# The convolutions' four-row tiles: DMA from SBUF to SBUF in place of copies on ScalarE and VectorE

## The chip, the cores and the metric

One Trainium2 chip, one of its cores. The metric is the device time of one execution in microseconds; the time before is the median of three runs. All numbers are in float32. Engines are called as in the profile: PE (TensorE), ACT (ScalarE), DVE (VectorE), POOL (GpSimd), SP (SyncE, which here issues DMAs).

## The reference

The input `x` is [8, 32, 128, 128] (images, channels, rows, columns). Four residual blocks follow each other, each adding a branch of the group-normalized input (`_gn` with 32 groups, so one mean and variance for each image and channel):

```python
x = x + L0(_gn(x))   # depthwise 11x11 Gaussian blur
x = x + L1(_gn(x))   # a gate
x = x + L2(_gn(x))   # snake convolution, 9 taps moved along y
x = x + L3(_gn(x))   # deformable 3x3 convolution with modulation
```

Three of them contain a dense 3x3 convolution over 32 channels, and the change is about these alone. L1 pads by wrapping, convolves 32 to 32 channels, and uses mean and variance of the result and of its SiLU to gate the input. L2 convolves 32 to 18 channels (`w_off`), normalizes in nine groups, takes tanh of it, and the first nine channels, summed up from the middle, move the sampling rows. L3 convolves 32 to 18 channels (offsets) and 32 to 9 (modulation, through a sigmoid and a mean); the offsets say where the input is sampled.

## The kernel before

The eight images are worked on in two groups g of four (`NG` = 2, `GI` = 4). SBUF has 128 partitions, and a group's `xn` holds the normalized input with image b's 32 channels on partitions 32b to 32b+31 and the padded rows behind each other along the free dimension: 130 rows of 130 floats in the gate stage, 136 of 136 (`HP`, `PAD` = 4) in the others. Each stage is a function with a block of its own, one program for each engine, and ends with a barrier of all engines, so stages don't overlap. In order: weights and tables, `blur`, `gate_conv` for both groups, `gate_scale`; then for each group `residual`, `snake_offsets`, `snake`, `residual`, `dcn_offsets`, and `dcn_dense` or its alternative. The convolution runs in three kinds of stage: `gate_conv` (gate), `snake_offsets` (snake) and `dcn_offsets` (dcn); two groups make six stages.

**The convolution (`RowConv`, L614 on).** A matmul contracts over partitions, and 32 channels would fill only a quarter of them. So for each image b two tiles of 128 partitions are filled, `low` and `high`, each of [128, 32, 130]: partition block q of `low` (32 partitions) holds the rows top-1+q, top+3+q, ... of the image, every fourth one, 32 in all, and `high` the rows two further down. With a weight tile of [128, 64] for each of three columns dx, one output row quad comes from six matmuls: `low` writes output partitions 0 to 63 (two rows of 32 channels), `high` 64 to 127. A unit u is 4 x 128 columns, one PSUM bank; an image has `NU` = 8 units, and four banks `acc` rotate. In float32 each matmul shows as two records in the trace, 592 ns each at the higher clock, started 0.43 us after each other; the ones of `low` and `high` run side by side. Both tiles exist twice (index b % 2), so the tiles of image b+1 are filled while image b is convolved, and those of image b+2 may not be touched before image b's convolution is over (`conv_done`, counted per unit).

**The filling (`move`, L636 to L647).** For each image eight copies of [32, 32, 130] floats from image b's 32 partitions of `xn` into one partition block of `low` or `high`. Three are done by ACT (`OF_ACT`; recorded at L663 in the helper `act_copy`) and five by DVE (`OF_DVE`; recorded at L647). The lists say behind which unit of the image before each copy stands in its engine's order of work; those of image 0 come at the stage's start. PE waits for both counts (`wait_moved`).

**Around it.** In the gate stage the input is loaded by SP (L705), measured and normalized by DVE and ACT, wrapped around by DVE (`padded`), and then convolved. ACT takes each unit out of PSUM with SiLU (L776) into one of four `hid` tiles, DVE measures it (L741).

In the snake stage ACT takes each unit out of PSUM (L1024) into `raw[b % 2]`, DVE measures it (L1071), and behind units 1 and 2 of the next image the group mean, variance and coefficients of image b are worked out; ACT does root, and the two halves of tanh (`squash`, L1015), behind units 2, 3 and 5 of image b+1. Then SP stores image b with four DMAs of 9 partitions each (L982), and before ACT writes unit 0 of image b+2 it waits for that store.

In the dcn stage ACT takes each unit out twice, as it is (L1768, into `cm`) and through a sigmoid (L1770, into `sig`), DVE takes the largest absolute value of each unit of `cm` (L1797), POOL adds the column numbers (L1786, `placed`), and SP stores each half image (four units) of `cm` with four DMAs of 18 partitions (L1824) and the half's mean of the modulation with four of 4 partitions (L1817). `cm`, `sig` and `mm` exist twice, by half: ACT waits for the store of half h before it writes the first unit of half h+2.

SP issues in its written order and waits in place: what stands behind a wait is issued later. In the snake stage it waits only for tanh, in the dcn stage for `placed` and the kept means.

Of the kernel before, what the change touches and what calls it, by code (L numbers as in the profile page):

```python
# [11 lines left out]
ACT = mybir.ActivationFunctionType  # L12
AX = mybir.AxisListType

B, C, H, W = 8, 32, 128, 128
P = 128
GI = P // C
# [598 lines left out]
class RowConv:  # L616
# [8 lines left out]

    OF_ACT = [((0, 0), 0), ((0, 1), 2), ((0, 2), 4)]
    OF_DVE = [((0, 3), 0), ((1, 0), 1), ((1, 1), 2), ((1, 2), 3), ((1, 3), 4)]

    def __init__(self, s, xn, top, left, w):
        self.xn, self.top, self.left, self.w = xn, top, left, w  # L630
        self.rows = [[s.sb(f"{n}{i}", [P, self.NI, W + 2]) for i in range(2)] for n in ("low", "high")]
        self.acc = [s.ps(f"acc{i}") for i in range(self.BANKS)]
        self.moved_act, self.moved_dve = s.sem("moved_act"), s.sem("moved_dve")
        self.conv_done = s.sem("conv_done")
# [3 lines left out]

    def move(self, eng, copy, moved, share, b, u=None):

        for (high, q), after in share:
            if u is not None and u != after:
                continue
            if b >= 2:
                eng.wait_ge(self.conv_done, (b - 1) * self.NU)
            r0 = self.top - 1 + 2 * high + q
            copy(self.rows[high][b % 2][C * q:C * q + C, :, :],  # L647
                 self.xn[C * b:C * b + C, r0:r0 + 4 * self.NI - 3:4, self.left - 1:self.left + W + 1]).then_inc(moved, 1)

    def wait_moved(self, pe, b):  # L650
        pe.wait_ge(self.moved_act, (b + 1) * len(self.OF_ACT))
        pe.wait_ge(self.moved_dve, (b + 1) * len(self.OF_DVE))

    def convolve(self, pe, b, u):
# [4 lines left out]
        ins.then_inc(self.conv_done, 1)  # L659


def act_copy(act):
    return lambda o, i: act.activation(o, i, ACT.Copy)  # L663


def gate_conv(nc, k, x1, g):
# [6 lines left out]
    with ExitStack() as ctx:  # L673
        s = Space(nc, ctx, f"gateconv{g}")
# [5 lines left out]
        conv = RowConv(s, xn, 1, 1, k.w_gate)  # L680
# [21 lines left out]
        @block.sync  # L702
        def _(sp):
            for l in range(NL):
                sp.dma_start(xg[:, l * LR:(l + 1) * LR, :], x1_v[:, l * LR:(l + 1) * LR, :]).then_inc(loaded[l], 16)  # L705

        @block.vector
        def _(dve):
# [25 lines left out]

            dve.wait_ge(padded, 1)
            conv.move(dve, dve.tensor_copy, conv.moved_dve, conv.OF_DVE, 0)
            for b in range(GI):
                for u in range(conv.NU):
                    v = b * conv.NU + u
                    dve.wait_ge(hid_ready, v + 1)  # L740
                    dve.bn_stats(hst[:, b, u, :], hid[v % 4][:, :]).then_inc(hid_used, 1)  # L741
                    if b + 1 < GI:
                        conv.move(dve, dve.tensor_copy, conv.moved_dve, conv.OF_DVE, b + 1, u)
            dve.wait_ge(hid_used, GI * conv.NU)
# [15 lines left out]
        @block.scalar  # L760
        def _(act):
            act.wait_ge(var_ready, 1)
            act.activation(std[:, :], mv[:, 1:2], ACT.Sqrt, bias=k.eps[:, :]).then_inc(std_ready, 1)
            act.wait_ge(coef_ready, 1)
            v = xg[:, 0:ACT_ROWS, :]
            act.activation(v, v, ACT.Identity, bias=k.norm1[:, g, 1:2], scale=k.norm1[:, g, 0:1]).then_inc(normed, 1)

            act.wait_ge(padded, 1)
            conv.move(act, act_copy(act), conv.moved_act, conv.OF_ACT, 0)
            for b in range(GI):  # L770
                for u in range(conv.NU):
                    v = b * conv.NU + u
                    act.wait_ge(conv.conv_done, v + 1)
                    if v >= 4:
                        act.wait_ge(hid_used, v - 3)
                    act.activation(hid[v % 4][:, :], conv.bank(b, u)[:, :], ACT.Silu, bias=k.vec('L1_conv_proj_bias')).then_inc(hid_ready, 1)  # L776
                    if b + 1 < GI:
                        conv.move(act, act_copy(act), conv.moved_act, conv.OF_ACT, b + 1, u)

# [168 lines left out]
def snake_offsets(nc, k, xn, steps, g):  # L948


    with ExitStack() as ctx:
# [25 lines left out]
        @block.sync  # L977
        def _(sp):
            for b in range(GI):
                sp.wait_ge(tanh_ready, 2 * b + 2)  # L980
                for q in range(4):
                    sp.dma_start(steps[:, b, q::4, :], raw[b % 2][32 * q:32 * q + 9, :, :]).then_inc(stored, 16)  # L982
            sp.wait_ge(stored, 64 * GI)
# [23 lines left out]
        def _(act):  # L1007
# [8 lines left out]

            conv.move(act, act_copy(act), conv.moved_act, conv.OF_ACT, 0)
            for b in range(GI):
                for u in range(NU):
# [6 lines left out]
                    if b > 0 and u in (2, 3, 5):  # L1026
                        (root, lambda x: squash(x, 0), lambda x: squash(x, 1))[(2, 3, 5).index(u)](b - 1)
                    if b + 1 < GI:
                        conv.move(act, act_copy(act), conv.moved_act, conv.OF_ACT, b + 1, u)
            root(GI - 1)  # L1030
# [4 lines left out]
        def _(dve):  # L1035
# [27 lines left out]

            conv.move(dve, dve.tensor_copy, conv.moved_dve, conv.OF_DVE, 0)
            for b in range(GI):
                for u in range(NU):
                    v = b * NU + u
                    if b > 0 and u in (1, 2):
                        (spread, coefficients)[u - 1](b - 1)
                    dve.wait_ge(raw_ready, v + 1)  # L1070
                    dve.bn_stats(st[b % 2][:, u, :], raw[b % 2][:, u * conv.UI:(u + 1) * conv.UI, :].rearrange("p i w -> p (i w)")).then_inc(stats_done, 1)  # L1071
                    if b + 1 < GI:
                        conv.move(dve, dve.tensor_copy, conv.moved_dve, conv.OF_DVE, b + 1, u)
                aggregate(b)
# [618 lines left out]
def dcn_offsets(nc, k, xn, offs, g):  # L1693


    with ExitStack() as ctx:
# [54 lines left out]
        def _(act):  # L1751
# [5 lines left out]

            conv.move(act, act_copy(act), conv.moved_act, conv.OF_ACT, 0)
            for b in range(GI):
                for u in range(NU):  # L1760
# [11 lines left out]
                    if v % HU == 3 and v > HU:  # L1772
                        keep_mean(half - 1)
                    if b + 1 < GI:
                        conv.move(act, act_copy(act), conv.moved_act, conv.OF_ACT, b + 1, u)
            keep_mean(2 * GI - 1)
# [12 lines left out]
        def _(dve):  # L1789
            conv.move(dve, dve.tensor_copy, conv.moved_dve, conv.OF_DVE, 0)  # L1790
            dve.wait_ge(columns_drawn, 1)
            dve.tensor_scalar(pos[:, :], pos[:, :], k.is_x[:, :], k.place3[:, :], ALU.mult, ALU.add).then_inc(pos_ready, 1)
            for b in range(GI):
                for u in range(NU):
# [3 lines left out]
                                      apply_absolute_value=True).then_inc(far_seen, 1)  # L1798
                    if b + 1 < GI:
                        conv.move(dve, dve.tensor_copy, conv.moved_dve, conv.OF_DVE, b + 1, u)  # L1800
            dve.wait_ge(far_seen, GI * NU)
# [9 lines left out]
        def _(sp):  # L1811
            def store_mean(half):
                sp.wait_ge(mean_kept, half + 1)
                b, r0 = half // 2, half % 2 * HR
                for j in range(HU):
                    rows = slice(4 * (r0 + j * UI), 4 * (r0 + (j + 1) * UI))
                    sp.dma_start(offs[MOD, b, rows, :].rearrange("(i q) w -> q i w", q=4), mm[half % 2][32 * j:32 * j + 4, :, :]  # L1817
                                 ).then_inc(mod_stored[half % 2], 16)

            for half in range(2 * GI):  # L1820
                sp.wait_ge(placed, (half + 1) * HU)
                b, r0 = half // 2, half % 2 * HR
# [496 lines left out]
```

## Time and profile before

| | us |
|---|---|
| time before, median of 3 runs | 3729.3 |
| lowest and highest | 3715.83, 3739.62 |
| profiled execution, its own time | 3735.51 |
| its span in the trace | 3733.5 |

The profiled execution is the one that all rows are from; its time lies 6 us above the median, and 2 us of it lie around the span. Rows of a timeline begin with the start in us from the span's start and a duration in us, and end in brackets with how long the engine had been idle and what released it; `x3` means three instructions merged into one row, `SPq` is SP's issuing of DMAs. A group row ends with busy us and the mean ns of one instruction, then the idle time before them. A row of a stretch has the stretch, its length, busy us and instructions of PE, PEld, DVE, ACT and POOL, the granted TensorE clock (1.00 is 2.4 GHz, 0.50 is 1.2 GHz), the mean busy share of the 16 DMA engines and the GB/s they moved.

### The profile page before, as it was taken

Reading aid. Unit: us, or ns where it says so; the run is one execution under the profiler, and the core shown is the slowest. Engines: PE = TensorE matmul, PEld = TensorE weight load, DVE = VectorE, ACT = ScalarE, POOL = GpSimd, SP = SyncE. Lnnn points to the kernel's source line nnn. Section 1 sums busy time; section 2 is a strip of 40 time slices with the busy share of each in tenths; the row PEclk is TensorE's granted clock in tenths of the full one; section 3 lists DMA queues with packets and bytes.
Section 4 is the critical chain, followed back from the end, with each engine's and each line's share of the span. In section 5 each row is a group of like instructions: output and inputs, shape, how many; then the busy total and the mean of one; then the engine's idle time right before and its main releaser. Section 6 shows DMA issues by size and latency. Waiting matters only on the chain. (4 is left out here: it accounts for less than half of the span.)

```text
span 3733.5 us, 86265 instructions
## 1 busy us (share of the span) xinstructions
PE 2749.0 (74%) x38569; PEld 1536.9 (41%) x38569; DVE 2064.7 (55%) x2867; ACT 1830.3 (49%) x1855; POOL 1090.2 (29%) x724
## 2 busy tenths in 40 slices
PE   1773753759999265888888828599990858888888
PEld 1762221226666121444444412366660224444444
DVE  5996677735555473454554465455545734545453
ACT  1113564735555373555555556455553835555544
POOL 0220001024443145333333210344421643343331
PEclk7886976879999677889889858799995968899889
DMA  2554114011111621212112141111117111121111
GB/s 55 145 139 122 39 52 180 7 25 25 31 25 25 233 75 48 63 60 67 56 60 67 51 187 13 27 23 31 25 25 276 38 50 63 59 68 58 61 63 44
DMA packets 213124, 257.74 MB, mean 69 GB/s; under 512 B 79188, under 2 KB 141192, under 8 KB 210696
## 3 DMA queue, kind: packets, MB, share of 16 engines
q1 hardware_dynamic: 203528, 218.58, 20.5%
q0 software_dynamic: 9216, 33.56, 2.2%
q8 instruction: 304, 4.98, 0.6%
q14 instruction: 76, 0.62, 0.1%
HBM read 153.52 MB, written 98.57 MB: 68 GB/s over the span
## 5 line engine op out<-in xcount | busy, mean ns | idle before, releaser
L2037 PE MATMUL dense_spread<-dense_cp,kept_spread_yx 32*128 32x512 f32 x2432 | 564.4, 729 | 229.8 <-DVE dense_cp L2194 149.2
L1308 ACT ACTIVATE snake_samp<-snake_s 128x1024 f32<-128x1024 f32 x320 | 321.2, 1023 | 359.1 <-PE snake_s L1237 358.9
L2156 ACT ACTIVATE dense_samp<-dense_s 128x864 f32<-128x864 f32 (+1 forms) x384 | 305.8, 829 | 331.2 <-PE dense_s L2084 331.0
L2208 DVE TENSOR_TENSOR dense_hat<-dense_spread,dense_hat 128x1024 f32<-128x1024 f32 x256 | 300.8, 1215 | 277.6 <-PE dense_spread L2037 277.6
L1371 DVE TENSOR_SCALAR snake_hat<-snake_spread 128x1024 f32<-128x1024 f32 x256 | 301.5, 1219 | 205.3 <-PE snake_spread L1215 205.3
L2136 ACT ACTIVATE dense_hat<-dense_spread 128x1024 f32<-128x1024 f32 x256 | 254.9, 1022 | 304.9 <-PE dense_spread L2037 298.2
L2084 PEld LDWEIGHTS dense_s<-dense_hat,dense_xt 64*64 64x64 f32 x11264 | 273.3, 135 | 193.7 <-issue 141.1
L1237 PE MATMUL snake_s<-snake_hat,snake_xt 64*64 64x128 f32 x10240 | 337.8, 274 | 19.1 <-ACT snake_samp L1308 18.8
L2096 PE MATMUL dense_s<-dense_samp,kept_w_dcn 64*64 64x264 f32 x4608 | 342.7, 457 | 2.8 <-ACT dense_samp L2156 2.8
L2084 PE MATMUL dense_s<-dense_hat,dense_xt 64*64 64x108 f32 x11264 | 327.9, 261 | 0.5
L2037 PEld LDWEIGHTS dense_spread<-dense_cp,kept_spread_yx 32*128 32x128 f32 x2432 | 149.0, 201 | 427.6 <-DVE dense_hat L2208 211.3
L657 PE MATMUL dcnoff_acc<-dcnoff_low,kept_w_off 128*64 128x512 f32 x384 | 174.1, 608 | 199.2 <-DVE dcnoff_high L647 194.2
L1237 PEld LDWEIGHTS snake_s<-snake_hat,snake_xt 64*64 64x64 f32 x10240 | 285.2, 134 | 85.7 <-issue 42.2
L657 PE MATMUL snakeoff_acc<-snakeoff_low,kept_w_off 128*64 128x512 f32 x384 | 184.1, 640 | 139.8 <-DVE snakeoff_high L647 139.8
L2096 PEld LDWEIGHTS dense_s<-dense_samp,kept_w_dcn 64*64 64x64 f32 x4608 | 194.6, 162 | 199.0 <-issue 137.8
L1186 POOL TENSOR_TENSOR snake_step<-xn 128x1240 f32<-128x1240 f32 (+1 forms) x64 | 176.3, 2754 | 319.6 <-DVE snake_xt L1363 310.1
L657 PE MATMUL gateconv_acc<-gateconv_low,kept_gate_w_gate 128*64 128x512 f32 x384 | 169.4, 604 | 118.6 <-DVE gateconv_high L647 118.6
L2017 POOL COPY dense_step<-dense_rows 128x176 f32<-128x176 f32 x64 | 32.4, 507 | 757.8 <-DVE dense_xt L2201 757.6
L2219 DVE TENSOR_TENSOR dense_mod<-dense_s,dense_mod 128x528 f32<-128x528 f32 x64 | 45.3, 708 | 369.8 <-PE dense_s L2096 369.8
L1252 PE MATMUL snake_s<-snake_samp,kept_w_dsc 64*64 64x256 f32 x4096 | 247.4, 379 | 0.2
L1215 PE MATMUL snake_spread<-snake_rw,kept_spread_y 32*128 32x256 f32 x2048 | 152.3, 413 | 69.9 <-DMA snake_rw<-steps 59.8
L1194 POOL TENSOR_TENSOR snake_xt<-snake_xt,kept_of_pair 128x1280 f32<-128x1280 f32 x64 | 148.5, 2320 | 169.3 <-ACT snake_xt L1302 169.3
(314 smaller groups left out, 4856.7 us busy)
## 6 DMA issues: line engine op xcount, KB each, us to landing
dense_cp<-offs SPq DMA_DIRECT2D x576, 56.0 KB
x<-blur_x SPq DMA_DIRECT2D x16, 1024.0 KB, 5.1
gateconv_xn<-x SPq DMA_DIRECT2D x16, 1024.0 KB, 11.0
pre<-snake_ob SPq DMA_DIRECT2D x32, 512.0 KB, 4.0
dense_xr<-x SPq DMA_DIRECT2D x64, 256.0 KB, 3.4
out<-dense_xr SPq DMA_DIRECT2D x64, 256.0 KB, 2.7
dense_cp<-offs SPq DMA_DIRECT2D x256, 48.0 KB
offs<-dcnoff_cm SPq DMA_DIRECT2D x64, 144.0 KB
```

The lines of the kernel that those rows point to most:

```text
L657: ins = pe.matmul(self.bank(b, u)[2 * C * high:2 * C * (high + 1), :], self.w[:, dx, :], self.rows[high][b % 2][:, u * self.UI:(u + 1) * s ...
L1186: pool.tensor_tensor(step[:, :, 0:n].rearrange("p x q -> p q x"), xn[:, r0 + 1:r0 + 1 + n, c0:c0 + SU], xn[:, r0:r0 + n, c0:c0 + SU], ALU. ...
L1237: ins = pe.matmul(banks[64 * j:64 * j + 64, bp, m * P:(m + 1) * P], xt[u % 2][r, v, :, :].rearrange("p b c -> p (b c)"), strided(hat[u % 2 ...
L1252: ins = pe.matmul(banks[64 * bp:64 * bp + 64, to, 0:256], k.w_dsc[r, t, r], samp[u % 2][r, bp, m0:m0 + SW // 2, slot, :], start=False, sto ...
L1308: act.activation(samp[u % 2][:, :, i * MS:(i + 1) * MS, :, :].rearrange("p b m t h -> p b (m t h)"), sample_at(u, i)[:, :, :], ACT.Copy).t ...
L1371: ins = dve.tensor_scalar(strided(hat[u % 2][:, 0:1], GUARD + (4 * tau + 2 * half) * SW * SR, [[8, 2], [SW * SR, 2], [SR, SW], [1, 8]]), s ...
L2037: return pe.matmul(bank[:, :], k.spread_yx[r, kind, :], cp[u % 2][r, tile, :], start=True, stop=True)
L2084: ins = pe.matmul(banks[64 * v:64 * v + 64, bp, at * PN:(at + 1) * PN], xt[u % 2][r, 2 * n + v, :, :].rearrange("p b c -> p (b c)"), hat[u ...
L2096: ins = pe.matmul(banks[64 * bp:64 * bp + 64, v, 0:2 * PC], k.w_dcn[r, t, r], strided(samp[r, bp, 0, SLOT[t], 0, 0:1], 0, [[PW, 2], [PN, N ...
L2136: act.activation(hat[u % 2][:, t:t + 2, :, 0:W].rearrange("p t r x -> p (t r) x"), p_hat[pair][:, :, :].rearrange("p t (r x) -> p (t r) x" ...
L2156: act.activation(samp[:, :, n0:n0 + nn, :, :, :].rearrange("p b n t r x -> p b (n t r x)"), sample_at(u, i)[:, :, 0:nn * PN], ACT.Copy).th ...
L2208: dve.tensor_tensor(h, p_hat[pair][:, :, :].rearrange("p t (r x) -> p (t r) x", x=W), h, ALU.mult).then_inc(main_ready, 1)
```

## The change

ACT's and DVE's copies are taken out everywhere, with `OF_ACT`, `OF_DVE` and `act_copy`. `move` now belongs to SP and issues eight DMAs from `xn` to the tiles, of the same shapes; each adds 16 to a semaphore of the tile's parity when it has landed, and PE waits for 128 times the number of images of that parity. For images 2 and 3 SP waits first for the convolution of the image two before. In the gate stage SP issues all four images in a row once `padded` is set. In the snake stage it issues images 0 and 1, then, for each b, image b+2 and then the waits and stores of image b. In the dcn stage it issues images 0 and 1, and before the stores of each odd half the image that is next.

```diff
-    OF_ACT = [((0, 0), 0), ((0, 1), 2), ((0, 2), 4)]
-    OF_DVE = [((0, 3), 0), ((1, 0), 1), ((1, 1), 2), ((1, 2), 3), ((1, 3), 4)]
...
-        self.moved_act, self.moved_dve = s.sem("moved_act"), s.sem("moved_dve")
+        self.moved = [s.sem(f"moved{i}") for i in range(2)]
...
-    def move(self, eng, copy, moved, share, b, u=None):
-
-        for (high, q), after in share:
-            if u is not None and u != after:
-                continue
-            if b >= 2:
-                eng.wait_ge(self.conv_done, (b - 1) * self.NU)
-            r0 = self.top - 1 + 2 * high + q
-            copy(self.rows[high][b % 2][C * q:C * q + C, :, :],
-                 self.xn[C * b:C * b + C, r0:r0 + 4 * self.NI - 3:4, self.left - 1:self.left + W + 1]).then_inc(moved, 1)
+    def move(self, sp, b):
+
+        if b >= GI:
+            return
+        if b >= 2:
+            sp.wait_ge(self.conv_done, (b - 1) * self.NU)
+        for high in range(2):
+            for q in range(4):
+                r0 = self.top - 1 + 2 * high + q
+                sp.dma_start(self.rows[high][b % 2][C * q:C * q + C, :, :],
+                             self.xn[C * b:C * b + C, r0:r0 + 4 * self.NI - 3:4, self.left - 1:self.left + W + 1]).then_inc(self.moved[b % 2], 16)
 
     def wait_moved(self, pe, b):
-        pe.wait_ge(self.moved_act, (b + 1) * len(self.OF_ACT))
-        pe.wait_ge(self.moved_dve, (b + 1) * len(self.OF_DVE))
+        pe.wait_ge(self.moved[b % 2], 128 * (b // 2 + 1))
...
@@ gate_conv, SP, behind the loads
+            sp.wait_ge(padded, 1)
+            for b in range(GI):
+                conv.move(sp, b)
...
@@ gate_conv, DVE (and the same on ACT, and in the other two stages)
-            dve.wait_ge(padded, 1)
-            conv.move(dve, dve.tensor_copy, conv.moved_dve, conv.OF_DVE, 0)
...
-                    if b + 1 < GI:
-                        conv.move(dve, dve.tensor_copy, conv.moved_dve, conv.OF_DVE, b + 1, u)
...
@@ snake_offsets, SP
+            for b in range(2):
+                conv.move(sp, b)
             for b in range(GI):
+                conv.move(sp, b + 2)
                 sp.wait_ge(tanh_ready, 2 * b + 2)
...
@@ dcn_offsets, SP
+            for b in range(2):
+                conv.move(sp, b)
             for half in range(2 * GI):
+                if half % 2 == 1:
+                    conv.move(sp, half // 2 + 2)
                 sp.wait_ge(placed, (half + 1) * HU)
```

## Rows read from the trace of the kernel before

**Rows 1.** The page: span, and busy time of each engine.
```profile
span 3733.5 us, 86265 instructions
...
PE 2749.0 (74%) x38569; PEld 1536.9 (41%) x38569; DVE 2064.7 (55%) x2867; ACT 1830.3 (49%) x1855; POOL 1090.2 (29%) x724
```

**Rows 2.** Chain that ended last, its first piece: start us, us, what.
```profile
3014.01 3.56 POOL dense_cp L1997 x2
```

**Rows 3.** Timeline of the first gate stage: start us, us, engine, line, operation [idle <-releaser].
```profile
348.66 11.05 ACT L663 ACTIVATE gateconv_low<-gateconv_xn 32x4160 f32<-32x4160 f32 x3 [1.04 <-DVE gateconv_xn L733]
...
348.66 2.32 DVE L647 COPY gateconv_low<-gateconv_xn 32x4160 f32<-32x4160 f32 x1
...
360.52 1.09 PE L657 MATMUL gateconv_acc<-gateconv_low,kept_gate_w_gate 128*64 128x512 f32 x1 [62.43 <-DVE gateconv_high L647]
...
444.16 0.69 DVE L741 BATCH_NORM_STATS2 gateconv_hid_stats<-gateconv_hid 128x6 f32<-128x512 f32 x1 [1.88 <-ACT gateconv_hid L776]
...
446.74 0.69 DVE L741 BATCH_NORM_STATS2 gateconv_hid_stats<-gateconv_hid 128x6 f32<-128x512 f32 x1 [1.88 <-ACT gateconv_hid L776]
```

**Rows 4.** Groups by line and shape: busy us, mean ns of one.
```profile
L663 ACT ACTIVATE gateconv_low<-gateconv_xn 32x4160 f32<-32x4160 f32 x24 | 88.1, 3670 | 2.6 <-DVE gateconv_xn L733 2.1
...
L647 DVE COPY gateconv_high<-gateconv_xn 32x4160 f32<-32x4160 f32 x32 | 74.2, 2318 | 1.0
...
L776 ACT ACTIVATE gateconv_hid<-gateconv_acc,kept_par 128x512 f32<-128x512 f32 x64 | 44.0, 687 | 59.4 <-PE gateconv_acc L657 58.0
...
L741 DVE BATCH_NORM_STATS2 gateconv_hid_stats<-gateconv_hid 128x6 f32<-128x512 f32 x64 | 43.8, 693 | 58.3 <-ACT gateconv_hid L776 57.4
```

**Rows 5.** Timeline of the first snake stage, in order of time.
```profile
667.53 1.08 PE L657 MATMUL snakeoff_acc<-snakeoff_low,kept_w_off 128*64 128x512 f32 x1 [66.16 <-DVE snakeoff_high L647]
...
715.33 5.78 SPq L982 DMA_DIRECT2D steps<-snakeoff_raw  x4
...
727.44 0.69 ACT L1024 ACTIVATE snakeoff_raw<-snakeoff_acc,kept_par 128x512 f32<-128x512 f32 x1 [10.99 <-DMA steps<-snakeoff_raw]
...
732.55 1.11 PE L657 MATMUL snakeoff_acc<-snakeoff_low,kept_w_off 128*64 128x512 f32 x1
...
738.46 0.59 PE L657 MATMUL snakeoff_acc<-snakeoff_low,kept_w_off 128*64 128x512 f32 x1
...
761.73 1.84 ACT L1024 ACTIVATE snakeoff_raw<-snakeoff_acc,kept_par 128x512 f32<-128x512 f32 x3 [10.87 <-DMA steps<-snakeoff_raw]
...
802.07 0.20 POOL L1173 MEMSET snake_hat<- 128x128 f32 x1 [155.18 <-POOLq L46]
```

**Rows 6.** Timeline of the first dcn stage, in order of time.
```profile
1328.25 3.76 ACT L663 ACTIVATE dcnoff_low<-xn 32x4160 f32<-32x4160 f32 x1 [0.95 <-PEq L46]
...
1370.88 0.69 ACT L1768 ACTIVATE dcnoff_cm<-dcnoff_acc,kept_par 128x512 f32<-128x512 f32 x1 [1.92 <-issue]
...
1395.02 0.69 ACT L1768 ACTIVATE dcnoff_cm<-dcnoff_acc,kept_par 128x512 f32<-128x512 f32 x1 [2.07 <-issue]
...
1401.58 17.08 POOL L1786 TENSOR_TENSOR dcnoff_cm<-dcnoff_cm,dcnoff_pos 128x512 f32<-128x512 f32 x7 [1.66 <-DVE dcnoff_far L1797]
...
1438.59 1.27 POOL L1786 TENSOR_TENSOR dcnoff_cm<-dcnoff_cm,dcnoff_pos 128x512 f32<-128x512 f32 x1 [2.45 <-DVE dcnoff_far L1797]
...
1418.69 3.26 SPq L1824 DMA_DIRECT2D offs<-dcnoff_cm  x4
```

**Rows 7.** Stretches while one DMA kind moves; last three columns: PEclk, DMA share, GB/s.
```profile
103.00:105.40 2.40, 1.11 (x10) 0.92 (x9) 2.26 (x22) 0.60 (x1) 0.00 (x0) 1.00 0.98 287
...
1388.50:1392.00 3.50, 3.10 (x18) 0.97 (x14) 2.62 (x4) 3.47 (x7) 3.50 (x3) 1.00 0.55 114
...
717.00:727.00 10.00, 4.07 (x20) 1.20 (x16) 0.57 (x2) 0.00 (x0) 0.00 (x0) 0.88 0.42 53
...
455.00:490.00 35.00, 0.00 (x0) 0.00 (x0) 22.67 (x36) 1.83 (x2) 0.00 (x0) 0.50 0.81 235
```

**Rows 8.** DMA issues: KB each, median us to landing.
```profile
snake_rw<-steps SPq DMA_DIRECT2D x64, 64.0 KB, 2.4
```

More of the change, by code:

```diff
@@ L659, in convolve @@
         ins.then_inc(self.conv_done, 1)
-def act_copy(act):
-    return lambda o, i: act.activation(o, i, ACT.Copy)
 def gate_conv(nc, k, x1, g):
@@ L766, in _ @@
             act.activation(v, v, ACT.Identity, bias=k.norm1[:, g, 1:2], scale=k.norm1[:, g, 0:1]).then_inc(normed, 1)
-            act.wait_ge(padded, 1)
-            conv.move(act, act_copy(act), conv.moved_act, conv.OF_ACT, 0)
             for b in range(GI):
@@ L776, in _ @@
                     act.activation(hid[v % 4][:, :], conv.bank(b, u)[:, :], ACT.Silu, bias=k.vec('L1_conv_proj_bias')).then_inc(hid_ready, 1)
-                    if b + 1 < GI:
-                        conv.move(act, act_copy(act), conv.moved_act, conv.OF_ACT, b + 1, u)
         @block.tensor
@@ L1015, in squash @@
                 act.activation(x, x, ACT.Tanh, bias=coef[:, b, 1:2], scale=coef[:, b, 0:1]).then_inc(tanh_ready, 1)
-            conv.move(act, act_copy(act), conv.moved_act, conv.OF_ACT, 0)
             for b in range(GI):
@@ L1027, in _ @@
                         (root, lambda x: squash(x, 0), lambda x: squash(x, 1))[(2, 3, 5).index(u)](b - 1)
-                    if b + 1 < GI:
-                        conv.move(act, act_copy(act), conv.moved_act, conv.OF_ACT, b + 1, u)
             root(GI - 1)
@@ L1062, in coefficients @@
                 dve.tensor_tensor(coef[:, b, 1:2], k.vec('L2_conv_gn_off_b'), d[:, c], ALU.subtract).then_inc(coef_ready, 1)
-            conv.move(dve, dve.tensor_copy, conv.moved_dve, conv.OF_DVE, 0)
             for b in range(GI):
@@ L1071, in _ @@
                     dve.bn_stats(st[b % 2][:, u, :], raw[b % 2][:, u * conv.UI:(u + 1) * conv.UI, :].rearrange("p i w -> p (i w)")).then_inc(stats_done, 1)
-                    if b + 1 < GI:
-                        conv.move(dve, dve.tensor_copy, conv.moved_dve, conv.OF_DVE, b + 1, u)
                 aggregate(b)
@@ L1756, in keep_mean @@
                 act.activation(mm[half % 2][:, :, :].rearrange("p i w -> p (i w)"), p_mean[half % 2][:, :], ACT.Copy).then_inc(mean_kept, 1)
-            conv.move(act, act_copy(act), conv.moved_act, conv.OF_ACT, 0)
             for b in range(GI):
@@ L1773, in _ @@
                         keep_mean(half - 1)
-                    if b + 1 < GI:
-                        conv.move(act, act_copy(act), conv.moved_act, conv.OF_ACT, b + 1, u)
             keep_mean(2 * GI - 1)
@@ L1789, in _ @@
         def _(dve):
-            conv.move(dve, dve.tensor_copy, conv.moved_dve, conv.OF_DVE, 0)
             dve.wait_ge(columns_drawn, 1)
@@ L1798, in _ @@
                                       apply_absolute_value=True).then_inc(far_seen, 1)
-                    if b + 1 < GI:
-                        conv.move(dve, dve.tensor_copy, conv.moved_dve, conv.OF_DVE, b + 1, u)
             dve.wait_ge(far_seen, GI * NU)
```

## The prediction

> **What bounds the kernel now.** The page first [rows 1]: no engine is full over the span (PE 74%, DVE 55%, ACT 49%), so the stages have different limits. The chain that ended last [rows 2] reaches back only to 3014 us, into the last dense stage; the stages end in barriers, and each has to be read by itself. The change touches six of them, three kinds, each once per group of four images.
>
> *Gate stage* [rows 3]. The copies of image 0 start at 348.7 (three on ACT, five on DVE, side by side), the first matmul starts at 360.5: 11.8 us of filling nothing overlaps. Then one tile of 512 columns ends every 2.58 us (444.16 to 446.74), 20.6 us per image. The ACT's own work per image is 8 x 0.69 + 3 x 3.67 = 16.5 us and DVE's 8 x 0.69 + 5 x 2.32 = 17.1 us [rows 4], both under 20.6: after image 0 the copies are hidden and PE is the bound.
>
> *Snake stage* [rows 5]. Twice, before images 2 and 3, ACT stands 11 us (727.44, 761.73), released by the store of the image two before, which uses the same raw buffer. The first such store is issued at 715.33 and done when ACT goes on at 727.44: 12.1 us for 4 x 144 KB. PE stops too, once four banks are full, and then runs slow: 1.11 us a matmul at 732.55, 0.59 at 738.46; that is the clock's lower level (1.2 GHz) after the idle time, six pairs at half pace, some 2.6 us lost. The stage lasts from 655.7 to 802.1, 146.4 us.
>
> *Dcn stage* [rows 6]. ACT is the bound: image 1's tiles start at 1370.88, image 2's at 1395.02, 24.1 us per image, more than PE's 20.6. From the first copy, 1328.25, to the last placed tile, 1438.59 + 1.27, are 111.6 us.
>
> **What the change removes.** 32 copies per stage, 192 in all: 72 on ACT and 120 on DVE, at 3.7 and at least 2.32 us each [rows 4] about 266 and 278 us of busy time. Little of it is on the path: the 11.8 us at each stage's start, in dcn some 3.5 us an image that ACT is slower than PE, and in snake some 7 us by which ACT's backlog delays the tanh and so the store: PE starts at 667.53 and needs 23.2 us for image 0, so image 1 starts at about 690.7; five more tiles at 2.58, the sixth and two halves of tanh would allow the store 17.5 us later, and it is issued 24.6 later, at 715.33 [rows 5]. DVE's copies also slow POOL: 17.08/7 = 2.44 us a tile beside them, 1.27 without [rows 6]; that goes as well, but POOL was not the bound.
>
> **What it adds.** Eight DMAs per image, 192 in all, on SP's queue. One moves 32 partitions x 32 rows of 520 bytes, 1,024 pieces; an image has 8,192 pieces, 4.26 MB, all from the same 32 partitions into 32 others at a time. I call the time of an image's eight D. Everything hangs on it, and the trace before has no copy from SBUF to SBUF. So I bound it by what a 512-byte piece costs a busy DMA engine [rows 7]: stores from 128 partitions, 98% of 16 engines, 287 GB/s: 512 x 16 x 0.98/287 = 28 ns; stores from 18 partitions (dcn), 0.55 of 16 engines, 114 GB/s: 40 ns; from 9 partitions (snake), 0.42 and 53 GB/s: 65 ns. The fewer partitions, the dearer a piece, although fewer engines are busy. I read that as engines sharing the way out of a few neighbouring partitions. With 8,192/16 = 512 pieces for each engine, D is 14 us at 28 ns, 20.5 at 40 and 33 at 65. The new DMAs touch 32 partitions, so 40 ns is the nearest row; I raise it to 47 ns, D = 24 us, because the pieces are 520 bytes at a pitch of 520 or 544, aligned to nothing, and both ends are narrow. A first byte to landing adds about 2 us (loads of 64 KB land in 2.4 [rows 8]). Issuing costs SP some 0.8 us a DMA (3.26/4 [rows 6]), 6.6 an image, and lies beneath D.
>
> The Trainium skill weighs against this. Its page "DMA: Bandwidth & Descriptors" (section "Why small descriptors are slow (HBM only)") says that copies between SBUF and SBUF escape the small-piece penalty, and by its section "Where 436 GB/s comes from" the page gives an estimate of 4.26/0.436 = 9.8 us per image, by which PE would wait for no image after the first; that is rival A at its far end. No row before shows such a copy, so whether it holds here is open.
>
> **The sum, from each stage's start.** The DMA queue is served in order. Image 0 lands at 2 + D = 26, against 11.8. PE needs 23.2 for it (20.6, and 2.6 of low clock) to 49.2; image 1's tiles land at 50. Image 2 may only be fetched when image 0's convolution is done.
> - Gate: image 2 lands at 49.2 + 2 + 24 = 75.2, image 3 at 99.2, its convolution ends at 119.8. Before, DVE takes up the last tile at 446.74, ACT's 0.7 us earlier: 446.0 - 348.7 = 97.3. +22.5.
> - Snake: SP issues image 2's DMAs, waits for tanh of image 0 (17.5 after image 1's start, as above, at 67.5), and its store stands behind them: 75.2 + 12 = 87.2. ACT, which waits for it, starts image 2 at 88; image 3's DMAs follow the store to 111.2, the store of image 1 ends at 123.2, ACT starts image 3 at 124. From there before took 802.1 - 761.7 = 40.4: 164.4 against 146.4, +18. The relief of ACT is in this sum; what is late next is the DMA queue.
> - Dcn: the stage buffers halves of an image, and a half's store takes 6 us (4 x 144 KB at 114 GB/s and the small ones). Queue: images 0 and 1 to 50, store 56, image 2 to 80, two stores to 92, image 3 to 116, store 122. Only then may ACT write the second half of image 2; 25.5 us more (5.6 for that half on ACT at 2 x 0.69 a tile, image 3's eight tiles at some 2.3, POOL's last 1.3) end at 147.5 against 111.6, +36. The wait on the store is queued on ACT ahead of all later tiles, and PE waits for their banks.
>
> Sum 76.5 per group, two groups, 153 us. The profiled execution took 3735.5 us (span 3733.5 and 2 around it), 6 above the median of 3729.3: 3888.5, rounded **3889 us**, 4% slower.
>
> **Rivals.** (A) *The narrow partitions bind less*, D of 10 to 17. Then, at D = 15: gate 17 + 85.5 = 102.5 (+5); snake's stores queue behind less, it ends at 139.7 (-7); dcn +5: +6 in all, 3742. At D = 10: gate 0, snake -11.5, dcn -1, together -25, 3711. For it: 28 ns is the price of a wide piece, also where it lands in SBUF rows at a pitch of 520 bytes (the gate's load: 512 x 16 x 0.81/235 = 28 ns [rows 7]). Against: the 40 and 65 ns rows. The point that decides is D = 17, where the sum crosses 37 us. This is the case that is not slower, and even it stays within 1%: the copies were nearly hidden.
> (B) *A piece costs as much as in the 9-partition store*, 65 ns and more, or half the engines take part: at D = 34 gate +61, snake +57, dcn +76, twice: +388, 4124. At D = 48, which is 47 ns with half the engines, the sum is +724, 4460. For it: the stores of 9 partitions show that neighbours can hold each other up that much, and here both ends are narrow. Against: the 18-partition row.
> (C) *The clock falls in the gaps.* Where PE stands 4 us or more between images, it may come back at the lower level, as at 732.55; 2.6 us each, at most 3 per stage: up to +47 on the forecast. Shorter gaps of 2 us (ACT's at 1395.02 [rows 6]) show no fall. This widens the range only. That the change does not do what it says I rule out: the copies are gone from the text, and the waits with them.
>
> **Chances.** Forecast (D 17 to 30, 3770 to 4030): 0.65. A: 0.17, most of it within 1%, 0.04 faster. B: 0.18. About 1%, 37 us, is what a measurement can tell from no change. Faster 0.04, same 0.13, slower 0.83. The range leaves out the far part of B and the better part of A: 3755 to 4125.
>
> **What would show it.** Right: the copies gone; SP's issues of low and high, 192, with the queue's share of 16 engines up by about 24 x 24 = 576 us, some 15% of the span; first matmul of a stage 26 us after its start; in the gate stage PE idle for about 4 us before images 2 and 3, ended by the DMA of low; in snake and dcn ACT waiting on stores that stand behind the moves; POOL's placing at 1.27 us a tile throughout. Wrong: a first matmul 12 to 17 us after the start (A), or over 34 (B); PE without gaps in the gate stage; or stores that land in 12 us though moves stand before them, which would mean that the queue isn't served in order.

## The result, and the profile after

The changed kernel takes 3928.3 us (median of 4 runs, 3925.6 to 3954.7) against 3731.1 (4 runs, 3715.8 to 3739.6) of the kernel before in the same comparison: 1.054 of it, with a 95% interval of 1.050 to 1.058. The forecast was 3889. The profiled spans are 3924.0 and 3733.5 us [rows 1], 190.5 apart, against 153 forecast.

The page of the kernel after: span, PE, SP's DMA queue (packets, MB, share of 16 engines), the gate stage's matmuls, and one of its six move groups:

```profile
span 3924.0 us, 86259 instructions
...
PE 2766.8 (71%) x38569; PEld 1529.9 (39%) x38569; DVE 1776.5 (45%) x2747; ACT 1564.1 (40%) x1783; POOL 1030.0 (26%) x724
...
q1 hardware_dynamic: 403208, 320.83, 32.5%
...
L654 PE MATMUL gateconv_acc<-gateconv_low,kept_gate_w_gate 128*64 128x512 f32 x384 | 179.8, 631 | 173.6 <-DMA gateconv_high<-gateconv_xn 173.6
...
gateconv_high<-gateconv_xn SPq DMA_DIRECT2D x32, 520.0 KB, 11.6
```

Here `...` stands for rows left out. DVE gave up 288 us and ACT 266 (278 and 266 forecast), and the span grew: the relief was off the path. The queue's share of the 16 engines' time rose from 20.5% (the page of the kernel before) to 32.5%, by 12 points where some 15 were forecast. The matmuls' releaser is now a DMA where it was DVE's copy [rows 3].

Timeline of the first gate stage after (start us, us, engine, line):

```profile
350.55 7.17 SPq L645 DMA_DIRECT2D gateconv_low<-gateconv_xn  x4
357.76 13.26 SPq L645 DMA_DIRECT2D gateconv_high<-gateconv_xn  x4
...
378.65 1.11 PE L654 MATMUL gateconv_acc<-gateconv_low,kept_gate_w_gate 128*64 128x512 f32 x1 [78.53 <-DMA gateconv_high<-gateconv_xn]
...
401.53 7.29 SPq L645 DMA_DIRECT2D gateconv_low<-gateconv_xn  x4
...
405.06 0.64 PE L654 MATMUL gateconv_acc<-gateconv_low,kept_gate_w_gate 128*64 128x512 f32 x1 [3.58 <-DMA gateconv_high<-gateconv_xn]
...
430.63 1.12 PE L654 MATMUL gateconv_acc<-gateconv_low,kept_gate_w_gate 128*64 128x512 f32 x1 [4.75 <-DMA gateconv_high<-gateconv_xn]
...
457.36 0.69 PE L654 MATMUL gateconv_acc<-gateconv_low,kept_gate_w_gate 128*64 128x512 f32 x1 [4.29 <-DMA gateconv_high<-gateconv_xn]
...
461.90 0.69 ACT L766 ACTIVATE gateconv_hid<-gateconv_acc,kept_par 128x512 f32<-128x512 f32 x1 [8.09 <-PE gateconv_acc L654]
```

The first matmul is 28.1 us after the first issue (before: 11.8). Four DMAs hold SP for 13.3 us (10.4 in long and 7.4 in wide, below, where the bytes move faster): past the first few, SP issues only as fast as the engines move, so the issues show the rate, 2 x 13.3 = 26.6 us an image. The landings of images 0 and 1 lie 26.4 us apart (378.65, 405.06). PE stops before every image, for 3.58, 4.75 and 4.29 us. After the first fill and the stop of 4.75 its matmuls begin at 1.11 us, the clock's lower level (1.2 GHz), and then take 0.59; after the stop of 3.58 they begin at 0.64.

First snake and first dcn stage after (they start at 722.40 and 1412.10):

```profile
799.10 7.47 SPq L973 DMA_DIRECT2D steps<-snakeoff_raw  x4
...
804.79 0.64 PE L654 MATMUL snakeoff_acc<-snakeoff_low,kept_w_off 128*64 128x512 f32 x1 [3.27 <-DMA snakeoff_high<-xn]
...
806.61 9.94 SPq L645 DMA_DIRECT2D snakeoff_low<-xn  x4
...
812.35 1.26 ACT L1014 ACTIVATE snakeoff_raw<-snakeoff_acc,kept_par 128x512 f32<-128x512 f32 x2 [10.11 <-DMA steps<-snakeoff_raw]
...
838.17 1.12 PE L654 MATMUL snakeoff_acc<-snakeoff_low,kept_w_off 128*64 128x512 f32 x1 [9.94 <-DMA snakeoff_high<-xn]
...
844.38 0.69 ACT L1014 ACTIVATE snakeoff_raw<-snakeoff_acc,kept_par 128x512 f32<-128x512 f32 x1 [15.41 <-DMA steps<-snakeoff_raw]
...
1503.44 0.69 ACT L1752 ACTIVATE dcnoff_cm<-dcnoff_acc,kept_par 128x512 f32<-128x512 f32 x1 [20.17 <-issue]
...
1509.04 6.77 SPq L645 DMA_DIRECT2D dcnoff_low<-xn  x4
...
1529.11 10.00 SPq L1807 DMA_DIRECT2D offs<-dcnoff_cm  x4
...
1542.79 0.69 ACT L1752 ACTIVATE dcnoff_cm<-dcnoff_acc,kept_par 128x512 f32<-128x512 f32 x1 [22.36 <-issue]
...
1571.75 1.27 POOL L1768 TENSOR_TENSOR dcnoff_cm<-dcnoff_cm,dcnoff_pos 128x512 f32<-128x512 f32 x1 [2.44 <-DVE dcnoff_far L1778]
```

In snake the wait at image 2 is no longer than before, but the one at image 3 is (15.41 us against 10.87 [rows 5]). In dcn ACT waited 2 us at images 1 and 2 before [rows 6]; now it waits 20 and 22 us, and at another place: before the second halves of images 1 and 2, for the store of the half two before. (Some of the expectations below put these waits at images 2 and 3.) A store of four DMAs that held SP for 3.26 us [rows 6] holds it for 10.00 behind the moves.

All kernels, by their first group's stages (us; first copy or move to the last evacuation by ACT in gate and dcn, to the last tanh in snake; each from the timeline of ACT and SP):

| kernel | gate | snake | dcn | whole, median | before beside it |
|---|---|---|---|---|---|
| before | 98.1 | 133.6 | 109.5 | 3731 | |
| after | 130.1 | 149.4 | 158.9 | 3928 | 3731 |
| wide | 102.7 | 127.5 | 117.7 | 3755 (one run) | 3721 |
| long (gate only) | 113.5 | 149.9 | 160.1 | 3908 (one run) | 3721 |
| aligned (gate only) | 111.9 | 146.7 | 158.4 | 3886 (one run) | 3721 |
| twoq | 128.5 | 147.1 | 157.5 | 3903 (one run) | 3721 |
| first_engines | 111.7 | 131.7 | 136.4 | 3808 | 3725 |
| stores_pool | 130.3 | 153.0 | 159.5 | 3936 | 3725 |
| stores_first | 130.2 | 146.8 | 156.2 | 3914 | 3725 |
| stores_off | 130.0 | 155.7 | 155.7 | 3921 | 3722 |
| hybrid | 96.8 | 124.3 | 106.4 | 3706 | 3725 |
| five | 96.6 | 124.3 | 115.9 | 3721 | 3722 |
| hybrid2 | 95.6 | 118.5 | 103.7 | 3689 | 3722 |

After minus before is 32.0 + 15.8 + 49.4 = 97.2, twice 194, close to the spans' 190.5. The same stage of the two groups differs by up to 5 us in snake and 2 in dcn, so smaller stage differences than that are not read. Totals of single runs are no finer: long and aligned differ by 23 us in the total and by 8 in the six stages together.

### The profile page after: what moved, and what is told of

It reads as the page before. It is cut to its first block and busy times, and to the rows that moved or that the text cites. A ratio compares the mean times of both kernels' runs of the same rounds, so it can differ in the third digit from the quotient of the medians.

```text
span 3924.0 us, 86259 instructions
## 1 busy us (share of the span) xinstructions
PE 2766.8 (71%) x38569; PEld 1529.9 (39%) x38569; DVE 1776.5 (45%) x2747; ACT 1564.1 (40%) x1783; POOL 1030.0 (26%) x724
## 3 DMA queue, kind: packets, MB, share of 16 engines
q1 hardware_dynamic: 403208, 320.83, 32.5%
## 5 line engine op out<-in xcount | busy, mean ns | idle before, releaser
L654 PE MATMUL dcnoff_acc<-dcnoff_low,kept_w_off 128*64 128x512 f32 x384 | 185.1, 639 | 288.6 <-DMA dcnoff_high<-xn 236.0
L654 PE MATMUL gateconv_acc<-gateconv_low,kept_gate_w_gate 128*64 128x512 f32 x384 | 179.8, 631 | 173.6 <-DMA gateconv_high<-gateconv_xn 173.6
L654 PEld LDWEIGHTS dcnoff_acc<-dcnoff_low,kept_w_off 128*64 128x64 f32 x384 | 54.1, 146 | 414.3 <-DMA dcnoff_high<-xn 238.0
```

Source lines behind the costliest of these rows:

```text
L654: ins = pe.matmul(self.bank(b, u)[2 * C * high:2 * C * (high + 1), :], self.w[:, dx, :], self.rows[high][b % 2][:, u * self.UI:(u + 1) * s ...
```

## What makes a move slow: four experiments

In the diffs `...` stands for code left out.

**wide.** Each DMA fills 8 rows of all 128 partitions instead of 32 rows of 32 partitions; pieces, their number and the bytes stay. It leaves out the shift between partitions, so the tiles hold other data; here and in the next two the choice between the dense and the general path is held at dense, the one that the real data take.

```diff
-sp.dma_start(self.rows[high][b % 2][C*q:C*q+C, :, :], self.xn[C*b:C*b+C, r0:r0+4*NI-3:4, ...])
+sp.dma_start(self.rows[high][b % 2][:, 8*q:8*q+8, :], self.xn[:, r0:r0+29:4, ...])
```

> The same eight DMAs an image with the same 8,192 pieces of 520 bytes, but each over 128 partitions and 8 rows in place of 32 partitions and 32 rows, each partition into itself (so the rows that the convolution reads are the wrong ones: which image and which of the four shifted rows stands in a block is left out). The test on the largest offset is set so that the dense path is always taken. Theory N (a piece is dear because 32 neighbouring partitions share their way out): the price falls to the 28 to 30 ns of the 128-partition rows; image 0 lands some 17 us after the first issue instead of 28, PE has no gaps after it in the gate stage, total about 3745. Theory P (the piece itself is dear: 520 bytes, aligned to nothing, both ends in SBUF): still 26 us an image, total 3928.

**long.** In the gate stage each DMA reads one run of 16,640 bytes per partition (other rows than the convolution wants), from the same 32 partitions.

```diff
-self.xn[C*b:C*b+C, r0:r0+4*NI-3:4, ...]
+self.xn[C*b:C*b+C, :, :].rearrange("p h w -> p (h w)")[:, o:o+NI*(W+2)]
```

> In the gate stage alone each DMA copies the same 16,640 bytes a partition from the same 32 partitions, but from one run of memory (the selection of every fourth row is left out there; the dense path is always taken). Snake and dcn are as in the changed kernel. Theory N (bytes through 32 partitions): an image takes nearly as long as now, 22 to 26 us, the first landing 24 to 28 us after the first issue. Theory P (pieces): with 1/32 of the pieces it comes near what wide transfers of long rows do, 393 GB/s, 11 us an image; first landing 13 us after the issue; total some 32 + 32 = 60 us under the changed kernel's.

**aligned.** In the gate stage pieces of 512 bytes, both ends at multiples of 512; the padding columns, and with them the shifted reads, are left out.

```diff
+self.xn[...].rearrange("p h w -> p (h w)")[:, o:o+4*W*NI].rearrange("p (i c) -> p i c", c=4*W)[:, :, 0:W]
```

> In the gate stage alone the pieces are 512 bytes, begin on multiples of 512 bytes in the source and fill a tile without gaps that begins on such a multiple (the two edge columns and the rows' shift are left out, PE reads the same columns three times; the dense path is always taken). Same 32 partitions, same count of pieces. If alignment and the odd 8 bytes are what lifts the price over the stores' 40 ns: 26 us an image falls to 20 to 22, first landing 22 to 24 us after the issue, stage 4 x 4 = 16 us shorter or more. If they are not: 26 less 1.5%, 25.6.

**twoq.** The high tile's DMAs of images 0 and 1 are issued from ACT's queue.

```diff
+conv.move(act, b, (1,))        # b = 0, 1; SP moves (0,) alone for these
```

> For images 0 and 1 of every stage the four DMAs of the high tile are issued by ACT's queue while SP issues the low ones; images 2 and 3 as before. Theory I (SP's issuing, which stands 3.3 us on each DMA, limits the rate, and the 16 engines are busy 0.83 of the time because of it): two queues bring image 0 in some 16 to 20 us in place of 28, and the stages get 8 to 12 us shorter each, 50 to 70 in all. If the engines or the way out of the partitions limit: image 0 and 1 together still take 52 to 54 us; PE's first matmul is not earlier than now by more than 2 us; total within 10 us of 3928.

What the sixteen DMA engines did from 352 to 366 us, when only moves run (the row's last two numbers: share of 16 engines, GB/s). After:

```profile
352.00:366.00 14.00, 0.00 (x0) 0.00 (x0) 0.00 (x0) 0.00 (x0) 0.00 (x0) 0.50 0.84 165
```

wide:

```profile
352.00:366.00 14.00, 0.00 (x0) 0.00 (x0) 0.00 (x0) 0.00 (x0) 0.00 (x0) 0.50 1.02 287
```

long, and the stretch to 372, which it needs to settle:

```profile
352.00:366.00 14.00, 0.00 (x0) 0.00 (x0) 0.00 (x0) 0.00 (x0) 0.00 (x0) 0.50 0.94 190
352.00:372.00 20.00, 0.00 (x0) 0.00 (x0) 0.00 (x0) 0.00 (x0) 0.00 (x0) 0.50 0.98 200
```

aligned:

```profile
352.00:366.00 14.00, 0.00 (x0) 0.00 (x0) 0.00 (x0) 0.00 (x0) 0.00 (x0) 0.50 0.82 201
```

twoq:

```profile
352.00:366.00 14.00, 0.00 (x0) 0.00 (x0) 0.00 (x0) 0.00 (x0) 0.00 (x0) 0.50 0.84 162
```

Three levels. Over 128 partitions the same pieces move at 287 GB/s, an image in 14.8 us, and the gate stage is 27 us shorter. From 32 partitions the best is 200, reached alike by long runs and by aligned 512-byte pieces: there the number of pieces costs nothing. Pieces of 520 bytes at an odd pitch take it down to 165. (aligned changes length and alignment together; which of the two counts stays open.) So the two ends' width and the pieces act together: neither alone gives 165. What the narrow end takes depends on what it is held against: 30% of wide's 287, or more than half of what 4 KB rows over 128 partitions reach in the kernel before, where loads and stores of `residual` run:

```profile
616.00:640.00 24.00, 0.00 (x0) 0.00 (x0) 23.65 (x31) 12.34 (x10) 5.32 (x10) 0.50 1.03 420
```

No run copies long rows between 128 and 128 partitions of SBUF.

A second queue changes nothing in the rate, so SP's issuing is not the limit. twoq's one run is 25 us under the change. Some 10 of these lie between the runs of the kernel before beside them (3721 and 3731); its stages differ from after's by 1.4 to 2.3 us each in the first group, less than two groups of one run do, and the rest isn't explained here.

The Trainium skill's page "DMA: Bandwidth & Descriptors" (section "Why small descriptors are slow (HBM only)") says that SBUF-to-SBUF copies escape the small-piece penalty. long against aligned agrees as to the count of pieces (200 and 201 GB/s); the level doesn't follow from it, since 32 partitions and 520 bytes gave 165. wide does not bear it out either: its 520-byte pieces took 29 ns of a busy engine (512 x 16 x 1.02/287), as long as the 512-byte pieces of stores from 128 partitions (28 [rows 7]).

The Trainium skill's page "SBUF — State Buffer" (section "Door 1: The DMA port swizzle (why `[64,N]` ≈ `[32,N]`)") bears on the level: partitions 0 to 31 reach 8 of 16 SBUF ports, 189 GB/s at 1 MiB and 218 at most, and only 128 partitions reach all. The traces agree: 200 and 201 from 32 partitions, against 287 and 420 over 128. By 218 GB/s an estimate for D is 4.26/0.218 = 19.5 us, just under the 20.6 us of the matmuls; the prediction did not use this page, and no run here brings the 520-byte pieces to that level.

Even wide isn't faster than the kernel before (gate +4.6, snake -6, dcn +8). It is the prediction's rival A as a run, and that sum's parts at D = 15 (gate 102.5 us, snake -7, dcn +5) lie close to it.

## Where the price lies: start, stores and amount

**first_engines.** Image 0 is filled by the copies of the kernel before, images 1 to 3 by DMA.

```diff
+conv.first(act=act)     # three ACT copies of image 0
+conv.first(dve=dve)     # five DVE copies of image 0
-for b in range(GI): conv.move(sp, b)
+for b in range(1, GI): conv.move(sp, b)
```

> Image 0 of each stage is filled by ScalarE's three and VectorE's five copies as in the kernel before, images 1 to 3 by the eight DMAs of the changed one. Theory A (a stage pays the whole latency of its first image, and then 26.6 us of moves against 20.6 us of matmuls for each later one): the first matmul comes 12 us after the stage can start instead of 28, image 1 has no gap (its moves run beside the copies and image 0), images 2 and 3 keep gaps of about 8 us in the gate stage; about -20 us in each of the six stages, 3790 to 3830 us. Rival B (the start is hidden or the copies slow down beside the DMAs, so that the fill of image 0 costs the same either way): less than 40 us gained, over 3880 us. What is left over 3729 us is the price of rate and stores alone.

3808.4 us, 1.021 of before (1.017 to 1.024): 3.3 of the change's 5.4 per cent, some 120 us, hang on the first fill of six stages (28.1 less 11.9 us six times is 97, the stop before image 1 the rest). First matmul and the next stop, in the first gate stage:

```profile
361.42 1.08 PE L689 MATMUL gateconv_acc<-gateconv_low,kept_gate_w_gate 128*64 128x512 f32 x1 [62.32 <-DVE gateconv_high L654]
...
411.70 1.12 PE L689 MATMUL gateconv_acc<-gateconv_low,kept_gate_w_gate 128*64 128x512 f32 x1 [7.50 <-DMA gateconv_high<-gateconv_xn]
```

11.9 us after the stage's start, and no stop before image 1. Gate keeps +14, dcn +27; snake is as long as before within what is read here.

**stores_pool, stores_first, stores_off.** Three ways to take the stores from behind the moves.

```diff
 # stores_pool (snake, dcn)
-sp.dma_start(offs[0:MOD, ...], cm[...])
+pool.dma_start(offs[0:MOD, ...], cm[...])
 # stores_first (dcn): the odd half's store ahead of the moves
-    if half % 2 == 1: conv.move(sp, half // 2 + 2)
     sp.wait_ge(placed, (half + 1) * HU)
     ...
+    if half % 2 == 1: conv.move(sp, half // 2 + 2)
 # stores_off: stores_pool, and behind ACT's copy of the means
+act.dma_start(offs[MOD, ...], mm[...])
```

> The stores of snake's steps and of dcn's offsets are issued from POOL's queue instead of SP's; the moves and the store of the modulation means stay on SP. Theory A (a store waits in the queue behind an image's eight moves, and SP, held in issuing the stores, starts the next image's moves late): ScalarE's waits at images 2 and 3 shrink, by about 8 us a snake stage and 10 to 20 us a dcn stage, 3875 to 3895 us. Rival B (the moves' rate alone sets when the next image can start, and the stores only stand beside it): within 12 us of the changed kernel's 3928. Rival C (POOL's own issues are slow and hold up its placing of dcn's tiles): over 3940.

> In the dcn stage alone, SP issues the stores of an image's second half before the moves of the image after the next, instead of behind them. Theory A (ScalarE's waits of 20.17 and 22.36 us at images 2 and 3 end with stores that stand behind the moves): each of these waits gets shorter by the 10 us or so that the second half's stores now leave earlier, less the 5 us by which the moves start later; 5 to 15 us a stage, 3900 to 3920. Rival B (these waits end with the moves themselves, which now start later): 3928 to 3945.

> As stores_pool, and in the dcn stage the means' stores, too, leave SP's queue: ScalarE issues them behind its own copy of the means. SP then issues moves alone in snake and dcn. Theory A (in dcn a store standing behind an image's moves ends ScalarE's waits; in stores_pool the means' store, left on SP, took the place of the offsets' store): what is left of the waits at images 2 and 3 is TensorE's wait for the moves, about 12 us each in place of 20 to 22, and the dcn stage takes 140 to 148 us instead of 159: 3890 to 3910 us. Rival B (the sixteen DMA engines are full, and it is all the same from which queue a store comes): the dcn stage stays at 155 to 160 us, 3925 to 3940.

Measured against before: 1.0555 (1.051 to 1.060), 1.051 (1.047 to 1.055) and 1.054 (1.051 to 1.056); the change alone is 1.054. None is told apart from it. In stores_pool's dcn stage the wait only changed its end, to the means' store that still stood behind the moves on SP:

```profile
1550.12 0.60 ACT L1745 ACTIVATE dcnoff_mm<-dcnoff_mean 128x512 f32<-128x512 f32 x1 [16.06 <-DMA offs<-dcnoff_mm]
```

In stores_off's dcn stage SP issues moves alone, and ACT waits for PE, which waits for the moves; ACT is also held in its own issues:

```profile
1495.17 5.84 ACTq L1749 DMA_DIRECT2D offs<-dcnoff_mm  x4
...
1551.58 0.69 ACT L1761 ACTIVATE dcnoff_cm<-dcnoff_acc,kept_par 128x512 f32<-128x512 f32 x1 [14.23 <-PE dcnoff_acc L654]
```

and PE's timeline of the same stage, image 1's first matmul:

```profile
1480.28 1.12 PE L654 MATMUL dcnoff_acc<-dcnoff_low,kept_w_off 128*64 128x512 f32 x1 [11.01 <-DMA dcnoff_high<-xn]
```

In the changed kernel it is this one:

```profile
1468.11 1.09 PE L654 MATMUL dcnoff_acc<-dcnoff_low,kept_w_off 128*64 128x512 f32 x1 [3.52 <-DMA dcnoff_high<-xn]
```

From the stage's start image 1 came at 63.4 us with the stores on other queues and at 56.0 without, though SP had issued its moves at the same time (the last of them ended at 47.7 and 47.6). So the order in the queue names the wait that the trace shows, and does not set the stage's length: moves and stores share the DMA engines, and a store taken out of the queue runs beside the moves and slows them. How much of stores_off's 155.7 us is ACT's standing on its issues is open.

**hybrid, five, hybrid2.** Image 0 by the engines; of images 1 to 3 a part by DMA. hybrid: ACT's three pieces. five: these and two of DVE's. hybrid2: hybrid, and of image 0 two pieces by DMA, two on ACT, four on DVE.

```diff
+BY_DMA = [(0, 0), (0, 1), (0, 2)]                      # hybrid, hybrid2
+BY_DMA = [(0, 0), (0, 1), (0, 2), (1, 2), (1, 3)]      # five
+for high, q in (self.BY_DMA if b > 0 else [(0, 2), (1, 3)]):   # hybrid2
```

> Image 0 by both engines; of images 1 to 3 VectorE copies its five pieces as before, and the three that ScalarE copied come by DMA from SP. Theory A (the DMA's rate is the bottleneck of the changed kernel: three pieces need about 10 us of the queue against 20.6 us of TensorE): no gap from moves is left, ScalarE has 11 us an image less to do, and the time is 3700 to 3735 us, the kernel before being 3729. Rival B (copies on VectorE run slower beside DMAs, or an order across two kinds of movers makes the last piece late): over 3745.

> As hybrid, but five pieces of images 1 to 3 come by DMA (ScalarE's three and VectorE's last two), and VectorE copies three. Theory A (DMA time per image decides, moves and stores added: five moves are 16.6 us at 26.6 us for eight; that is under the 20.6 us of matmuls in the gate stage and under a snake image, but in dcn the stores' 12.8 us of SP's queue per image come on top, 29 us against 24 us an image): gate stage 97 us as in hybrid, snake 124 to 130, dcn 112 to 125 instead of 106; 3720 to 3745 us. Rival B (only the moves count, and 16.6 us is hidden everywhere): within 6 us of hybrid's 3706.

> As hybrid, but image 0 is split three ways: ScalarE two pieces, VectorE four, and two by DMA. Theory A (the copies of image 0, 11 us on ScalarE and 11.6 on VectorE, set the start; two DMAs land about 7 us after their issue): the first matmul comes 9.3 us after the stage can start instead of 11.8, 2.5 us in each of six stages, 3688 to 3698 us. Rival B (the two DMAs land later than the copies end, or the time comes back later in the stage, where snake waits for its stores): 3702 us or more.

hybrid: 3705.9 us (8 runs), 0.994 of before (0.992 to 0.996). five: 3720.6, 0.9995 (0.998 to 1.001). hybrid2: 3688.8 (6 runs), 0.992 (0.990 to 0.995). In the first group gate and snake are the same with three and five pieces; dcn is 9.5 us longer with five. The waits of ACT there, five:

```profile
1381.74 0.69 ACT L1796 ACTIVATE dcnoff_cm<-dcnoff_acc,kept_par 128x512 f32<-128x512 f32 x1 [10.81 <-issue]
...
1411.03 0.69 ACT L1796 ACTIVATE dcnoff_cm<-dcnoff_acc,kept_par 128x512 f32<-128x512 f32 x1 [14.40 <-issue]
```

and hybrid:

```profile
1374.05 0.69 ACT L1796 ACTIVATE dcnoff_cm<-dcnoff_acc,kept_par 128x512 f32<-128x512 f32 x1 [3.73 <-PE dcnoff_acc L689]
...
1397.14 0.69 ACT L1796 ACTIVATE dcnoff_cm<-dcnoff_acc,kept_par 128x512 f32<-128x512 f32 x1 [3.93 <-PE dcnoff_acc L689]
```

Before, the stores of an image hold SP for 12.8 us (2 x 3.3 for `cm` and 2 x 3.1 for the means). Three moves (10 us) and these fit beside 24 us an image; five (16.6) do not, though 16.6 alone is under PE's 20.6. This is the amount as cause, by a change of size: 3, 5 and 8 pieces give dcn stages of 106, 116 and 136 (first_engines). hybrid2's first gate stage:

```profile
349.88 0.71 SPq L674 DMA_DIRECT2D gateconv_low<-gateconv_xn  x1
...
359.35 1.08 PE L690 MATMUL gateconv_acc<-gateconv_low,kept_gate_w_gate 128*64 128x512 f32 x1 [59.81 <-DVE gateconv_high L654]
```

9.5 us from start to first matmul instead of 11.8, released by DVE's fourth copy: the two DMAs were in by then. It is the fastest kernel measured here.

## Why the prediction was right, and where its terms were off

The time lies in the forecast's range, 39 us above its value, and the mechanism is the forecast one: a first fill that nothing overlaps, and then moves that come slower than PE works. That the total came so near is in part luck: the errors below have both signs.

- *The copies were nearly hidden, so their removal buys little.* Right. hybrid puts a size on it: with ACT's copies gone and their DMAs hidden, snake is 9.3 us shorter in the first group and dcn 3.1; gate is not told apart (1.3 shorter in the first group, 1.1 longer in the second). The medians differ by 19 us. In the forecast's snake I had counted 7 for ACT's backlog.
- *D = 24 us, at 47 ns a piece.* The term that was mis-sized, by a tenth: 26.6 us. By the prediction's reckoning a piece took 512 x 16 x 0.84/165 = 42 ns of a busy engine, near the 40 of the row that I chose; but I had let D follow from the busy time as if no engine would idle, and they idled 16% of it: per wall time a piece took 26.6/512 = 52 ns. Of my two reasons for the raise above 40, the narrow ends alone do not bear it out (aligned: 512 x 16 x 0.82/201 = 33 ns), and neither do the 520-byte pieces alone (wide: 29 ns); together they gave the 42.
- *The sum with the measured D.* With D = 26.6 the prediction's own sum (image 2 now has to wait for the queue, so the landings are at 2 + 3D and 2 + 4D) gives gate +31.7, snake +27.2 and dcn +46.3, 210 us for two groups. Measured were +32.0, +15.8 and +49.4: gate and dcn follow from D, snake does not.
- *Gate +22.5.* Measured +32.0. By the forecast's own marks from the stage's start: first matmul 28.1 (26), image 0 done and image 2's moves issued 51.0 (49.2), image 2 landed 80.1 (75.2), PE's first matmul of image 3 at 106.8 (99.2), end 129.4 to 130.1 (119.8). Each landing is later by the D that stands in it; 1.9 at the end are matmuls at the lower clock.
- *Snake +18.* Measured +15.8, which is luck: two errors cancel. ACT goes on at 90.0 (88) and 122.0 (124), as if the marks held. But I had let a store take 12 us behind the moves, and the next moves start behind the store. PE began image 2 at 82.4 and image 3 at 115.8, so ACT went on only 7.6 and 6.2 us behind the moves: moves and a store overlap in part. Image 3's moves were issued from 84.2 on, while the first store was still under way. This gave back what the longer D took.
- *Dcn +36.* Measured +49.4. ACT begins the second half of image 1 at 91.3, where the forecast's queue has its store done at 86 (the 92 there is the end of the store after it). Image 3's moves are issued at 96.9 (92). ACT begins the second half of image 2 at 130.7 (122), and the end is at 160.9 (147.5). The four D's ahead of that mark, 2.6 more each, would give 10.4 for the 8.7 measured there; the tail is 30.2 instead of 25.5, since image 3's tiles came at PE's 2.58 us or more each, not at ACT's 2.3. That the store's place in the queue is the cause I had argued, and that did not hold up: with no store on SP the stage was 3 us shorter, where the expectation had 11 to 19.
- *Rival A* (D of 10 to 17, at or under no change) needed 128 partitions. wide's D of 14.8 gave 34 us more than the one run of the kernel before beside it, 20 by the two spans that the traces have, and 13 in the stages of the first group taken twice; I had worked out 6 for 15. *Rival B* did not come. *Rival C*, the clock in the gaps, came beside the forecast: by the stretches of the two traces the first group's busy PE time grew from 85.5 to 88.6 us in gate and from 94.0 to 99.6 in dcn with the same matmuls, not in snake: 18 us for both groups. How much of it lies on the path was not measured.

## What to carry to other kernels

Before moving hidden copies to a DMA queue, add the DMA's time per image, stores included, and hold it against the bound of the stage; move as many pieces as fit under it (three of eight here) and leave the rest on the engines. What no work precedes, a stage's first fill, is to be split over all movers so that they end together. That a wait ends with a store behind moves in one queue does not show that their order costs the time: it does once a run without that order is shorter.

## What the runs showed of the hardware

- SBUF to SBUF: 287 GB/s over 128 partitions with 520-byte pieces (wide), 165 with the same pieces from 32 into 32 (after), and 200 from 32 into 32 with aligned 512-byte pieces or long runs (aligned, long).
- A DMA's issue is no fixed cost. Four moves hold SP 13.3 us, four small stores 3.3 alone and 10.0 behind moves; on ACT four issues of 8 KB each stood 5.84 us beside moves and 1.30 when none ran (stores_off).
- Stores on another queue run beside the moves and delay them: image 1 of dcn came 7.4 us later (stores_off).
- Engine copies did not suffer from moves beside them: three on ACT took 11.06 us in first_engines and 11.05 before [rows 3].
